# The first half of a mixture of experts run inside the tail of the attention before it, weight preparation split up, and a shorter inverse square root

## The reference

```python
# differential attention: two softmaxes, window of 64, 16 heads, 4 kv heads
diff = relu(p1 - lam * p2);  diff = diff / (diff.sum(-1) + 1e-06);  out = (diff @ v) @ Wo
# mixture: 8 experts of 176, 4 groups, the best 2 groups, then the best 2 experts, and a shared expert of 352
scores = softmax(h @ gate_weight.T);  topk_w, topk_i = _group_limited_topk(scores)
e = einsum('ntf,nhf->nth', silu(g) * u, down_w);  routed = einsum('nth,tn->th', e, wmat)
out = routed + silu(h @ sh_gate_w.T) * (h @ sh_up_w.T) @ sh_down_w.T
# binary weights: sign(w) * mean(|w|) a row; ternary: scale = mean(|W|) + 1e-8, clip(round(W/scale), -1, 1) * scale
# layer norm: (x - m) / sqrt(v + 1e-05)
```

## Time and profile before

| | |
|---|---|
| time, median of 3 runs | 1120.84 us (1119.29 to 1123.8) |
| profiled execution | 1121.06 us |
| its span, first to last instruction | 1119.3 us |
| mean granted TensorE clock | 0.916 |
| busy TensorE, VectorE, ScalarE, GpSimd | 985.6, 708.7, 532.2, 333.6 us |

### The profile page before, as it was taken

One profiled execution on the slowest core, in us unless ns is written; L12 is line 12 of the kernel. 1 busy time (PEld: TensorE's weight loads), 2 busy tenths in 40 slices (PEclk: granted clock), 3 DMA queues, 4 the chain that ended last, 5 costly groups with the idle time before them and its releaser, 6 DMA issues. The chain is left out here.

```text
span 1119.3 us, 16501 instructions
## 1 busy us (share of the span) xinstructions
PE 985.6 (88%) x5914; PEld 564.0 (50%) x5914; DVE 708.7 (63%) x2007; ACT 532.2 (48%) x1141; POOL 333.6 (30%) x464
## 2 busy tenths in 40 slices
PE   6999998988989868999999999996879988988795
PEld 2544544775445534356365544443546444445584
DVE  1667774877897965323323567778461777876685
ACT  3566665434787833100112556663443445556331
POOL 3311113331786850000002211121110346662442
PEclk8989999898897978899998989998888978999897
DMA  6000000101003002000000020000000000000000
GB/s 239 1 1 1 1 1 1 52 1 39 1 19 131 2 1 111 0 1 1 0 1 1 1 113 1 1 1 1 1 1 1 1 1 1 2 1 1 1 14 25
DMA packets 4325, 21.61 MB, mean 19 GB/s; under 512 B 377, under 2 KB 1657, under 8 KB 3220
## 3 DMA queue, kind: packets, MB, share of 16 engines
q1 hardware_dynamic: 4244, 20.55, 4.9%
HBM read 19.01 MB, written 1.05 MB: 18 GB/s over the span
## 5 line engine op out<-in xcount | busy, mean ns | idle before, releaser
L961 ACT ACTIVATE PB<-pair 128x1024 f32<-128x1024 f32 (+3 forms) x288 | 223.1, 811 | 139.6 <-PE pair L1722 138.4
L1217 DVE CUSTOM_DVE_ANT_0 junk<-bank,cst 128x128 bf16<-128x128 f32 (+3 forms) x384 | 171.0, 487 | 110.2 <-PE bank L1706 107.6
L793 POOL TENSOR_SCALAR_AFFINE_SELECT PB<-PB 128x256 f32<-128x256 f32 x192 | 79.0, 414 | 323.7 <-ACT PB L961 321.8
L1220 DVE TENSOR_REDUCE pmx<-bank 128x1 f32<-128x512 f32 x192 | 122.6, 685 | 52.0 <-PE bank L1706 51.3
L1706 PE MATMUL bank<-KO_r,QO_r 64*128 64x512 f32 (+3 forms) x576 | 143.1, 422 | 10.6 <-DVE A L1295 4.9
L1738 PE MATMUL pvb<-PB,V 128*32 128x512 f32 (+3 forms) x1152 | 126.1, 510 | 11.9 <-ACT PB L961 8.5
L1706 PEld LDWEIGHTS bank<-KO_r,QO_r 64*128 64x128 f32 x576 | 74.0, 193 | 111.7 <-DVE pmx L1217 40.5
L1718 PE MATMUL pair<-QO_r,KO_r 64*128 64x512 f32 (+3 forms) x576 | 115.9, 393 | 11.8 <-ACT PB L961 10.6
L799 POOL TENSOR_TENSOR parts_r<-y_f,parts_r 128x512 fp32r<-128x512 f32 x24 | 30.7, 1279 | 317.6 <-ACT parts_r L932 317.6
L1722 PE MATMUL pair<-ms,sel_r 64*128 64x512 f32 (+3 forms) x576 | 102.1, 347 | 0.0
L1032 ACT ACTIVATE KO<-pair,nm 128x128 f32<-128x128 f32 x256 | 89.9, 395 | 9.2 <-DVE nm L1380 9.1
(11 more groups left out here) (222 smaller groups left out, 1709.4 us busy)
## 6 DMA issues: line engine op xcount, KB each, us to landing
WF<-in_moe_gu SPq DMA_DIRECT2D x1, 3520.0 KB, 12.4
WA<-in_w_att SPq DMA_DIRECT2D x3, 1024.0 KB, 6.2
WF<-in_tern_w SPq DMA_DIRECT2D x1, 3072.0 KB, 10.0
V<-in_moe_d SPq DMA_DIRECT2D x1, 1792.0 KB, 7.1
xT<-in_xT SPq DMA_DIRECT2D x2, 512.0 KB, 5.8
X<-in_x SPq DMA_DIRECT2D x1, 1024.0 KB, 10.7
A<-in_rope SPq DMA_DIRECT2D x1, 1024.0 KB, 4.7
out<-X SPq DMA_DIRECT2D x2, 512.0 KB, 2.9
```

The costliest lines, as they stand in the source:

```text
L793: pool.affine_select(p2, p2, pattern=[[0, 2], [1, P]], compare_op=ALU.is_ge, fill=0.0, base=0, channel_multiplier=-1).then_inc(causal, 1)
L961: act.activation(pb[:, st % 2, 2 * i:2 * i + 2, 0:n], ps[:, :, 0:n], ACT.Exp, scale=scale)\
L1217: r_done(dve.tensor_tensor_reduce(junk[:, (r_used - 1) % 3, 0:n], ps[:, 0:n], tri[:, HALF - n:HALF], 1.0, LOWEST, ALU.add, ALU.max, accum_ ...
L1220: r_done(dve.tensor_reduce(to, ps[:, 0:n], AX.X, ALU.max))
```

## The change

Nine edits go together.

1. The windowed attention finishes half 1 first: `OUT_FIRST[WATT]` is 1, and tile 4 comes fourth in `UNITS` in place of last. The last tile's uT lies in KO.
2. The norm of half 1, its transposition ("xout", now read by VectorE in place of ScalarE), the logits and the routing of this half are put into steps 25 to 32; chunks 0 to 7 of the mixture's first half into steps 32 to 40, beside the last units' transpositions and the last tile's pieces.
3. The tail has the norm of half 0, chunks 8 to 27, the second half's transposition at chunk 10, its routing in three parts behind chunks 11, 12 and 13, and both down projections at the end.
4. `route` and `ranked` work on one half (4 tiles) and are called twice, each in three parts. `moe` as a function of its own is gone on all engines.
5. The selector is loaded to WA[0] earlier and cast to `parts`; w_att2 is loaded to WA[0] behind that cast.
6. "weights" 0 and 1 stand behind "norm" and "new" of s = 4; 2 and 3 behind the last accT but one, 4 behind the last, 5 in the plan of s = 6 ahead of "late" 0. Before, 0 and 1 stood ahead of accT of the mixed stage, 2 to 5 ahead of a later one.
7. GpSimd waits for `tern_scale` when it takes its first ternary piece, not ahead of the whole of s = 6.
8. The late rows of q in the windowed attention are spread by one a step over steps 10 to 17.
9. The inverse root has one operation for its first guess in place of two and seven in place of nine to refine it.

```diff
-OUT_FIRST = {ATT: 1, GLU: 1, WATT: 0, MOE: 0, BIN: 1, TERN: 1}
+OUT_FIRST = {ATT: 1, GLU: 1, WATT: 1, MOE: 0, BIN: 1, TERN: 1}
...
-        plan[7:7] = [("late", k) for k in range(TH)] + [("late_norm",)]
+        plan[7:7] = [("weights", 5)] + [("late", k) for k in range(TH)] + [("late_norm",)]
     if s == 4:
-        for stage, items in ((STAGES[-3], range(2, 6)), (MIXED, range(2))):
-            at = plan.index(("accT",) + stage)
-            plan[at:at] = [("weights", n) for n in items]
+        for n, behind in ((0, ("norm",)), (1, ("new",)), (2, ("accT",) + STAGES[-2]), (3, ("weights", 2)),
+                          (4, ("accT",) + STAGES[-1])):
+            plan.insert(plan.index(behind) + 1, ("weights", n))
...
-UNITS = tiles(TH + 1, TH + 2, TH + 3) + tiles(0, 1) + tiles(2) + tiles(3) + tiles(TH)
+UNITS = tiles(TH + 1, TH + 2, TH + 3) + tiles(TH) + tiles(0, 1) + tiles(2) + tiles(3)
...
+    late.update({10 + 2 * g + x: q_late[g][x:x + 1] for g in range(NG) for x in range(TWO)})
+    mixture = {27: [("norm", 0, 2)], 28: [("xout",)], 29: [("logits", 0), ("route", 0, 0)], 31: [("route", 0, 1)],
+               32: [("gate", 0), ("up", 0)], 33: [("gate", 1), ("up", 1), ("sel",)], 34: [("gate", 2), ("up", 2), ("wT", 0)],
+               35: [("weighted", i) for i in range(3)]}
+    mixture.update({36 + i: [("gate", 3 + i), ("up", 3 + i), ("weighted", 3 + i)] for i in range(5)})
+    mixture[25], mixture[26] = [("norm", 0, 0)], [("norm", 0, 1)]
...
+        if k == len(UNITS):
+            plan += [("route", 0, 2)]
...
+        plan += mixture.get(k, [])
...
+    tail = [("norm", 1, 0), ("norm", 1, 1), ("norm", 1, 2)]
+    at = {MIX_X + 1: [("logits", 1), ("route", 1, 0)], MIX_X + 2: [("route", 1, 1)], MIX_X + 3: [("route", 1, 2)]}
+    for i in range(8, 2 * NF_MOE):
+        if i == MIX_X:
+            tail.append(("xin",))
+        tail += [("gate", i), ("up", i)] + [("wT", 1)] * (i == NF_MOE) + [("weighted", i)] + at.get(i, [])
+    tail += [("down", 0), ("post", 0), ("down", 1), ("xnew",), ("post", 1)]
...
-                    load(selF[:, :], t_in["sel"], ld_sel)
                     load(wd_moe, t_in["moe_d"], ld_moed)
                     load(WA[1][:, :], t_in["w_att3"], ld_att3)
+                    sp.wait_ge(cast_ready, 3)
+                    load(WA[0][:, :], t_in["w_att2"], ld_att2)
...
                     sp.wait_ge(xn_ready, 2 * NT)
-                    load(WA[0][:, :], t_in["w_att2"], ld_att2)
+                    load(selF[:, :], t_in["sel"], ld_sel)
...
-                    step(dve.tensor_scalar(y.bitcast(I32), v.bitcast(I32), 1, None, ALU.logical_shift_right))
-                    step(dve.tensor_scalar(y.bitcast(I32), y.bitcast(I32), -1.0, float(0x5F3759DF), ALU.mult, ALU.add))
+                    step(dve.tensor_scalar(y.bitcast(I32), v.bitcast(I32), -0.5, float(0x5F3759DF), ALU.mult, ALU.add))
                 if 1 in which:
-                    for _ in range(3):
-                        refine()
+                    step(dve.tensor_tensor(w, y, y, ALU.mult))
+                    step(dve.tensor_tensor(w, w, v, ALU.mult))
+                    step(dve.scalar_tensor_tensor(w, w, -10.0 / 3.0, w, ALU.add, ALU.mult))
+                    step(dve.scalar_tensor_tensor(y, w, 5.0, y, ALU.add, ALU.mult))
+
+                    step(dve.scalar_tensor_tensor(w, y, -0.5 * CUBIC ** 3, y, ALU.mult, ALU.mult))
+                    step(dve.tensor_tensor(w, w, v, ALU.mult))
+                    step(dve.scalar_tensor_tensor(y, w, 1.5 * CUBIC, y, ALU.add, ALU.mult))
...
+                if part == 0:
+                    ps = r_slot()[:, 0:TH * EXPERTS].rearrange("p (t e) -> p t e", t=TH)
+                    step(dve.tensor_reduce(top, ps, AX.X, ALU.max))
+                    r_done(dve.tensor_tensor(logit, ps, top.unsqueeze(2).to_broadcast([P, TH, EXPERTS]), ALU.subtract))
...
+                if part == 1:
+
+                    dve.wait_ge(pv_done, PV0[MIXTURE - 1] + NT - 1)
+                    dve.wait_ge(logit_exp, k + 1)
+                    step(dve.tensor_reduce(top, e, AX.X, ALU.add))
+                    step(dve.reciprocal(inv, top))
+                    step(dve.tensor_tensor(score, e, inv.unsqueeze(2).to_broadcast([P, TH, EXPERTS]), ALU.mult))
+                    step(dve.tensor_reduce(best[:, :, 0:4], grouped(score), AX.X, ALU.max))
+                    in_group = ranked(best[:, :, 0:4], 4, C_LOW4, ts)
...
+                if part == 2:
+                    chosen = ranked(e, 8, C_LOW8, ts)
```

More of the change, by code:

```diff
@@ L473, in windowed_plan @@
             plan.append(("outT", step[4]))
[L474 to L478, removed]
+        plan += mixture.get(k, [])
[6 more added lines that the diff above has]
+    tail += [("down", 0), ("post", 0), ("down", 1), ("xnew",), ("post", 1)]
+    kinds = [("uT", len(UNITS))] + [(kind, NT) for kind in ("pv", "acc", "accT", "outT", "proj")] \
+        + [(kind, 2 * NF_MOE) for kind in ("gate", "up", "weighted")]
+    assert all((plan + tail).count((kind, n)) == 1 for kind, top in kinds for n in range(top))
     return early, before, plan + tail
@@ L1048, in ffn @@
                     fc = i % nf
[L1049 removed]
                     ps = e_slot()
[L1052 removed]
+                    act.activation(sg[:, i % 4, :], ps[:, 0, :], ACT.Silu, scale=gate_scale(fc))\
                         .then_inc(e_free, 1)
@@ new lines, in windowed @@
+                    if item[0] == "logits":
+                        half = halves_in(MIXTURE)[item[1]]
+                        if item[1]:
+                            x_ready(half)
+                        else:
+                            pe.wait_ge(r_free, x_out_at[0])
+                        ps = r_slot()
+                        for k in range(TH):
+                            t = half * TH + k
+                            last = over_width(ps[:, k * EXPERTS:(k + 1) * EXPERTS], lambda c: xT[:, c, t * P:(t + 1) * P],
+                                              lambda c: cst[:, C_GW + c * EXPERTS:C_GW + (c + 1) * EXPERTS])
+                        last.then_inc(r_full, 1)
@@ new lines, in windowed @@
+                    if item[0] == "wT":
+                        half = halves_in(MIXTURE)[item[1]]
+                        pe.wait_ge(wm_ready, item[1] + 1)
+                        ps = r_slot()[0:3 * NEXP1, :].bitcast(BF16)
+                        for k in range(TH):
+                            last = pe.transpose(ps[:, k * P:(k + 1) * P],
+                                                wp[:, half * TH + k, :, :].rearrange("p k e -> p (k e)"), idb[:, :])
+                        last.then_inc(r_full, 1)
+                        pe.wait_ge(cast_ready, 3)
+                        wT_at.append(r_used)
@@ new lines, in windowed @@
+                    if item[0] == "down":
+                        half = halves_out(MIXTURE)[item[1]]
+                        h = hid[halves_in(MIXTURE).index(half)]
+                        if item[1] == 0:
+                            pe.wait_ge(ld_moed, 16)
+                            pe.wait_ge(r_free, r_used)
+                        for t in range(TH):
+                            if item[1] and t == TH // 2:
+                                new_x(MIXTURE, halves_out(MIXTURE)[0])
+                            ps = r_slot()
+                            at = t * P
+                            for fc in range(NF_MOE):
+                                n = mixture_rows(fc)
+                                last = pe.matmul(ps[:, 0:D], h[0:n, fc, at:at + P], wd_moe[0:n, fc, :],
+                                                 start=(fc == 0), stop=(fc == NF_MOE - 1))
+                            last.then_inc(r_full, 1)
```

309 lines of the change are left out of this document (129 added, 180 removed).

## The result

The changed kernel takes 1091.47 us (median of four executions of 1079.05 to 1092.54) against 1120.07 before (four of 1117.41 to 1123.8): a ratio of 0.9722, 95% interval 0.9657 to 0.9788. The forecast was 1092.5. The profiled execution of the changed kernel is its fastest one, 1079.05 us; a second profile, of an execution of 1092.79 us, stands beside it here, because the difference between the two turned out to matter.

What follows compares the result with a forecast made beforehand. TensorE, busy 88% of the span, was taken as the bound, losing time to waits and the slow clock behind them. Terms 13 + 11 + 4 = 28 off 1120.84 gave 1092.8, rounded to 1092.5 us; range 1083 to 1106.

Steps and rivals of the forecast that it cites:

- the likeliest case: Whole kernel: the forecast of 1092.5 us holds, own range 1088 to 1098, chance 0.48.
- Term A: Last windowed score tile to next attention: running the mixture into the tail cuts 199.8 us to 186.6, saving 13.
- Delay of the last score tile: End of the windowed score tiles: work put before the last tile on full VectorE delays it 5.0 us, ends 0 and 9.
- TensorE empty once: Behind the last score tile: TensorE idles 3.5 us while VectorE does its own work and routing, ends 0 and 7.6.
- collisions: Around the last score tile: VectorE operations with two inputs collide with GpSimd's subtraction, 1.5 us before it, 1.0 behind.
- The second half's weights: Mixture behind chunk 13: routing part 2 before the weights' transposition outlasts TensorE's work by 1.9 us, ends 0 and 4.
- steps with mixed shapes: Mixture inside the tail: nine steps alternating matmuls of different shapes cost some 0.2 us each, 2.0 together, ends 0 and 5.
- Term B: Ternary and binary weights' preparation: moving it removes TensorE's 7.4 us wait and more, saving 11 us, ends 4 and 12.
- The cover: Later attention: the moved ternary sums fit in gaps of 5.08 and 4.46 us; rival without cover, 1099.5 us, chance 0.10.
- Term C: Norms: nine small operations for twelve save 0.6 us each at seven of sixteen norms, 4 us, ends 2.5 and 5.
- rival with VectorE as the bound: Mixture in the tail: added VectorE operations and hand-overs cost more, its saving is 4 us, time 1102, chance 0.19.
- the other side: Nine mixed steps: TensorE waits over 3.1 us per step, making the kernel slower, 1137 at 5 us, chance 0.05.

Runs made afterwards that it cites:

- mixture_only: The changed kernel with the old placing of the weights' preparation and the old norms, so only the mixture moved into the tail: 1108.7 us, ratio 0.9882.
- ternary_only: The kernel before with only the ternary sums and their scale moved, the five binary operations left in place: 1107.25 us, ratio 0.9899.
- weights_only: The kernel before with only the weights' preparation moved, both plans and GpSimd's wait as in the change: 1103.58 us, ratio 0.9843.
- norms_longer: The kernel before with seven small operations, results unused, added to each norm: 1130.9 us, ratio 1.0089.
- norms_only: The kernel before with only the shorter inverse root in the norms: 1105.05 us, ratio 0.9839.

## Why the prediction was right, and where its sizes were off

**The time.** 1091.47 against 1092.5, inside the range and inside the likeliest case's own range. The two signs that would have shown the prediction wrong did not appear: TensorE's waits between 400 and 450 sum to 4.3 us and not to over 12, and the clock in the first 23.9 us is 0.93 and 0.86 and not near 0.7. That the parts came together to 28.6 us is in part luck, as the last paragraph here shows.

**Term A, 13: measured 13.8** (13.2 by the ratio, 11.4 to 15.0) for this part alone. Its marks: first gate product at 398.6 and 405.2 in the two profiles (near 406), next attention's first product at 578.8 and 584.4 (near 586). The last score tile ended at 395.5 and 402.1, before the 403 to 406 that was said; only in mixture_only, with the old norms, it was 405.6. The terms:
- The stretch behind the last score tile, which the working gives as 181.6 without the delay: 183.3, 182.3, and 183.4 in mixture_only.
- Delay of the last score tile, 5.0: the 32 units took 130.5 us against 126.2 at the same clock of 0.87, 4.3 more. In mixture_only they took 131.8, but at 0.85, so not all of those 5.6 is delay. The fastest profile has 124.4 at 0.91, where the old order had 122.2 at 0.92 (ternary_only): the delay is nearer 2 there. VectorE being full came about less than said: in the last 20.5 us of score tiles it is busy for 18.9 at a clock of 0.92, and in the second profile for 16.9 of the last 21.0 at 0.75, against 19.5 of 20.5 before. The items of this term sum to 7.0 and not 6.9.
- TensorE empty once, 3.5: 3.86. The working's own numbers give more than it took: 11.2 less 7.3 is 3.9. Parts 1 and 2 of the routing took 2.57 and 3.77 us against 2.75 and 3.8, without the 1.0 for collisions, and what ends the wait is the copy of u (L1490), which stands just ahead of the residual that the text names.
- The second half's weights, 1.9: 1.23, and 0.82 behind it for which the profile shows no release.
- The 2.0 for steps with mixed shapes was not measured by itself. The text's work at full clock less what moved, 174.2, plus the two waits is 179.3; the stretch is 4.0 and 3.1 us longer, and in it are this term, other short waits and the half clock behind the waits (1.7 for the one gate product).

What the text did not say is what term A is made of. Its 177.1 was worked out at full clock, so it gives back all slow clock of the stretch. The windows divide the 16.5 us by which the stretch became shorter: TensorE's free time fell from 13.2 to 7.9, which is 5.3, and its busy time from 186.6 to 175.5, which is 11.2, of which 2.9 is work moved ahead and the other 8 goes with the clock (0.93 to 0.98). More than half of this term's net gain is clock, which fits that at an equal clock it measures 5.0 by the fit.

**Term B, 11: the mechanism was right, the size is 8.2 at an equal clock by the fit,** 6.5 for the ternary part (8.8 less 0.3, of which 2.0 was clock) and 1.7 for the binary (2.5); TensorE's free time fell by 10.4. Taken back, it costs 6.7. Alone it measured 18.9, of which 8 to 11 is its own time and the rest came with the clock (0.912 to 0.927). The cover held, as the sums' timeline shows. The first binary projection starts 5.9 us behind its norm in place of 14.0, 8.0 sooner where about 9 was said. The question of what the weights' sums do to GpSimd's masks beside them is answered by weights_only: the two at 793.38, wholly beside the first two sums, took 0.385 us each, the two at 790.62 0.45, against 0.427 in the mean from 700 to 790. The Trainium skill (SBUF — State Buffer, Who interferes with whom) says that on trn2 a tensor_reduce never contends; the trace agrees, as far as these masks show it.

**Term C, 4: 4.2 alone and 5.0 taken back, at an equal clock.** Alone it measured 17.5 in plain times, over four times the term; the rest came with the clock (0.912 to 0.930). 0.60 a norm was exact. 13.6 for 1.4 a norm in norms_longer gives nearer ten norms on the path than seven; but a longer norm also uncovers waits that a shorter one does not have (four waits for X became seven).

**The collisions** were estimated too high, in the direction of the rival with VectorE as the bound. The product of 128x4 takes 0.269 us in the mean (346 to 402, second profile), against 0.427 before; that VectorE's work has moved against GpSimd's is my explanation, and no run tests it. That rival (A of 4) is out, and so is the other side: the gate products of the last five steps start 3.85 to 4.91 us apart (420.8 to 438.1, the longest with a projection between), and there TensorE has no wait over 0.2 us.

**The sum was right partly for another reason than its working says, and partly by luck.** At an equal clock the three terms are 17.5 and not 28; 28 contains about 10 of clock (8 in A, 2 in B), counted where the trace of before showed it. The clock gave some 14 in the whole kernel. Beyond those two stretches the prediction has nothing on the clock's level, and nothing in it says that the level would stop where it did: with the norms alone the plain gain was 13.5 us above the term. That 10 stood in the sum where some 14 came is luck as well as working, and one would be wrong to count the clock again for each part alone.

## What to carry to other kernels

Before adding up terms, split each into TensorE's free time and its busy time at the granted clock: the first adds over the parts of a change, the second need not. When a small edit gains several times its own time, look at the mean clock of every execution before looking for a mechanism, and compare at one clock. A chain that runs alone is worth filling with independent matmuls of the next stage, and what then decides is where VectorE's extra work stands in its queue ahead of the chain's copies: pulling two pieces of it apart removed a wait of 3.9 us and left one of 1.3 in another place.

## What the runs showed of the hardware that was not expected

- One kernel, unchanged, takes 1079.05 to 1094.43 us with a mean granted clock of 0.944 to 0.926; the kernel before takes 1109.70 to 1126.28 with 0.929 to 0.910. About 7.7 us for each 0.01, over 101 executions of the kernel before and eleven others.
- The level depends on the program and is not a simple function of how long TensorE waits: three operations fewer in each norm and seven more both raised it (medians, from 0.912 to 0.930 and to 0.919). What sets the level was not found. The Trainium skill (TensorE: Matmul & The Clock Gate, Part 1) says that the monitor behind the clock runs free of the program, so that one kernel shows different slow stretches from run to run; the levels of norms_only (0.936 and 0.918 to 0.923) agree with that, and no run here shows the cause itself.
- A stretch of 32 units with the same instructions took 122.2, 126.2 and 130.3 us as its clock was 0.92, 0.87 and 0.81.
